# A graph network on one core: the relation rows are stored after the next turn's first fetches, and x is fetched after the edge lists

## The reference

```python
x = _layernorm(x + _L0_gnn_ref(...))   # attention over 4 heads
x = _layernorm(x + _L1_gnn_ref(...))   # mean of messages, own term, relu, norm
# layer 2: softmax over the edges that leave a node, weighted sum at the target
e = ei_all[idx_i] + ej_all[idx_j]
e = jnp.where(e > 0, e, 0.01 * e)
alpha = _segment_softmax(e, idx_j, n)
out = relu(jax.ops.segment_sum(alpha[:, None] * x[idx_j], idx_i, n))
x = _layernorm(x + out)
# layer 3: a matrix for each of 4 relations, maximum at the target, own term
hr = x_src @ weight[r] + bias[r]        # r = relation of the edge
agg = jax.ops.segment_max(msg, dst, n)
x = _layernorm(x + (x @ weight[-1] + bias[-1] + agg))
```

## Time and profile before

| | us |
|---|---|
| runs: median of 3 (lowest, highest) | 4865.99 (4858.77, 4874.44) |
| profiled execution, its own time | 4846.01 |
| its span | 4844.2 |
| busy in the span: PE, DVE, ACT, POOL | 2474.6, 2187.0, 836.0, 3265.1 |
| second part of layer2 | about 2866 to 3684 |
| edge_lists | 0 to about 56 |

### The profile page before, as it was taken

The page is one execution under the profiler, slowest core; times in us unless marked ns, Lnnn a source line. Parts: engine busy times, 40 slices in busy tenths (PEclk is TensorE's granted clock), DMA queues, the critical chain, the costliest instruction groups (busy, mean ns, idle before and its releaser), DMA issues. The chain is left out here.

```text
span 4844.2 us, 67984 instructions
## 1 busy us (share of the span) xinstructions
PE 2474.6 (51%) x17617; PEld 2281.1 (47%) x17617; DVE 2187.0 (45%) x5635; ACT 836.0 (17%) x2497; POOL 3265.1 (67%) x3391
## 2 busy tenths in 40 slices
PE   1555555554344444443999986655654333333331
PEld 1444444443333333332999985544543333333331
DVE  4555555554122222223666666656653222222224
ACT  0122222221000000000444430000001111111112
POOL 2777777775777777774677776444432777777775
PEclk7555555555555555555555556666666555565565
DMA  4333333332222223232566666555553444444453
GB/s 106 80 82 81 80 80 80 81 81 53 54 55 55 55 55 56 55 55 58 175 179 183 178 203 201 174 187 171 168 183 94 130 130 130 130 132 132 132 132 95
DMA packets 421571, 550.23 MB, mean 114 GB/s; under 512 B 110747, under 2 KB 280175, under 8 KB 421343
## 3 DMA queue, kind: packets, MB, share of 16 engines
q1 hardware_dynamic: 306098, 319.68, 21.7%
q0 software_dynamic: 108064, 223.24, 20.6%
q10 hardware_dynamic: 7344, 6.61, 0.4%
HBM read 412.21 MB, written 138.30 MB: 114 GB/s over the span
## 5 line engine op out<-in xcount | busy, mean ns | idle before, releaser
L521 POOL DMA_INDIRECT G<-table,IC x2496 | 2367.3, 948 | 896.4 <-issue 787.3
L2397 POOL DMA_INDIRECT G<-table,IC x832 | 839.6, 1009 | 526.5 <-issue 370.5
L1358 PE MATMUL PS<-SEL,G 128*128 128x96 f32 x1664 | 384.2, 426 | 534.5 <-DMA G<-table,IC 528.1
L1358 PEld LDWEIGHTS PS<-SEL,G 128*128 128x128 f32 x1664 | 362.4, 330 | 557.2 <-issue 550.9
L2801 DVE TENSOR_TENSOR_SCAN GW<-BIG,GW,PS 128x512 f32<-128x512 bf16 x208 | 266.2, 1280 | 780.9 <-PE PS L2776 771.2
L1030 PE MATMUL PS<-SEL,GW 128*128 128x96 f32 x1664 | 385.9, 426 | 405.7 <-DVEq L1093 405.7
L1030 PEld LDWEIGHTS PS<-SEL,GW 128*128 128x128 f32 x1664 | 360.8, 329 | 415.3 <-DVEq L1093 415.3
L2776 PE MATMUL PS<-IDENT,G 128*128 128x128 f32 x832 | 204.7, 428 | 680.3 <-DMA G<-table,IC 680.3
L2776 PEld LDWEIGHTS PS<-IDENT,G 128*128 128x128 f32 x832 | 163.2, 223 | 717.1 <-DMA G<-table,IC 528.5
L2405 PE MATMUL PS<-BIG 128*128 128x49 f32 x1680 | 377.6, 412 | 1.1 <-ACT BIG L2345 1.1
L2405 PEld LDWEIGHTS PS<-BIG 128*128 128x128 f32 x1680 | 371.3, 334 | 1.2 <-ACT BIG L2345 1.2
(11 more groups left out here) (309 smaller groups left out, 3894.5 us busy)
## 6 DMA issues: line engine op xcount, KB each, us to landing
running_max<-BIG SPq DMA_DIRECT2D x105, 512.0 KB
GW<-source_in_block SPq DMA_DIRECT2D x209, 256.0 KB
G<-table,IC POOLq DMA_INDIRECT x3328, 2.5
rows_ahead<-G SPq DMA_DIRECT2D x104, 512.0 KB
ROWSF<-edge_places SPq DMA_DIRECT2D x209, 192.0 KB
BIG<-run_mask SPq DMA_DIRECT2D x104, 256.0 KB, 4.6
ROWSF<-rows_ahead SPq DMA_DIRECT2D x26, 512.0 KB
SELTF<-rows_ahead SPq DMA_DIRECT2D x26, 512.0 KB, 6.4
```

What stands on the lines that cost most here:

```text
L521: pool.indirect_dma_start(out=G[:, b, u, 0:width], out_offset=None, in_=table, in_offset=bass.IndirectOffsetOnAxis(ap=IC[:, b * U + u:b * ...
L1358: last = t.matmul(PS[q][:, 0:W], G[:, b, u, 0:D], SEL[:, q, u, :], start=u == 0, stop=u == U - 1)
L2397: pool.indirect_dma_start(out=GS[:, b, u, :], out_offset=None, in_=T2, in_offset=bass.IndirectOffsetOnAxis(ap=IC[:, b * U + u:b * U + u + ...
```

## The change

Two edits. In `edge_lists` ACT waits until the four edge-list tiles have landed before it fetches x. In the second part of `layer2` the store of a chunk moves from the end of its turn to the middle of the next one, behind that turn's groups 0 and 1 and its spills; the last chunk is stored after the loop. The two stores of a chunk and the wait ahead of them are the same as before.

```diff
@@ edge_lists, ACT
                     act.wait_ge(x_in, 48)
+                    act.wait_ge(rows_in, 64)
                     act.dma_start(XBUF[:, 0:N], xT).then_inc(x_in, 16)
@@ layer2
-            def sp_laps(sp, first, end, nodes0, nodes1):
+            def sp_laps(sp, first, end, nodes):
...
                             if b == 1:
                                 for j in range(2):
                                     spill(sp, lap * 4 + 52 + 2 * h + j, 2 * h + j, lap + 13)
-                        if (nodes0, nodes1)[h]:
-                            n, blk = chunk_of(turn)
-                            store_rows3(sp, S, n, blk, 2)
+                                if nodes:
+                                    n, blk = chunk_of(lap * 2 + h - 1)
+                                    store_rows3(sp, S, n, blk, 2)
...
-                        sp_laps(sp, 0, 1, False, False)
-                        sp_laps(sp, 1, 2, False, True)
-                        sp_laps(sp, 2, 13, True, True)
+                        sp_laps(sp, 0, 2, False)
+                        sp_laps(sp, 2, 13, True)
+                        store_rows3(sp, S, CHUNKS - 1, LEFT - 2, 2)
                         sp.wait_ge(S.stored, 32 * CHUNKS + 32)
```

## The result

| | before | after |
|---|---|---|
| runs: median (lowest, highest), us | 4863.99 (4858.77, 4874.44) | 4669.68 (4666.10, 4672.76) |
| after / before, 95% interval | | 0.9598 (0.9586 to 0.9610) |
| profiled execution, us | 4846.01 | 4666.10 |

The medians are 194.3 us apart, the two profiled executions 179.9 us (that of before lies 12.8 us under the quickest of its four runs, that of after is the quickest of its own). The changed kernel has one line more ahead of layer2, so L2498 of before is L2499 here, L890 is L891, L936 is L937.

What follows compares the result with a forecast made beforehand. Bound: DVE's own chain plus a list fetch queued on SP behind the wait for that chain's end. 182.3 - 4.5 + 4.2 = 182.0 us saved, set against the 4866.0 median: 4684 us, range 4652 to 4730.

Steps and rivals of the forecast that it cites:

- (a): Second part of layer2: with the list of group 0 issued earlier, all 22 list waits go, 182.3 us gained.
- (f): Lap ends in layer2: a jump hidden by the wait now shows, 0.41 x 11 = 4.5 us lost.
- (e): DVE's L890 in layer2 waits for PE's relation products: no change taken, bounds 44 us lost to 19.3 gained.
- (c): Layer2, row fetch and list of group 2 now behind the store: no cost, at least 1.9 us in hand.
- (d): Layer2 spills go out later, at about 3244: no cost, POOL has nearly 5 us in hand.
- (g, 0.73 forecast: Layer2, more bytes in less time: DMA engines' share rises from 0.55 to 0.73, cost taken as 0.
- x (4.2 us): edge_lists, x fetched later: SP passes the padding wait at 14.0 instead of 18.2, 4.2 us gained, between 0 and 5.4.
- need the same 10.8 us: edge_lists: after the padding the four lists take as long as before, 10.8 us (18.20 to 29.01).
- rival 1: PE's clock stays low in layer2, L890 waits 2.9 us every turn: saving falls to 138, 4728 us; chance 0.10.
- (2): Layer2, POOL cannot gather while its next spill lands: turns of 27.3 us, 132 saved, 4734 us; chance 0.06.
- (3): Layer2, group 2's list behind the store's wait comes too late: slower, 4939 us at a 22 us landing; chance 0.04.
- (4): Layer2, group 0's list waits for something else, say the buffer half; only the x edit counts: 4862 us; chance 0.03.

Runs made afterwards that it cites:

- The x experiment: Changed kernel with x fetched once the padding has landed, beside the list loads: 0.9681 of the kernel before on the slow chip; DVE starts on the lists at 30.09 us.

## Why the prediction was right, and which steps were off

**The list waits (a): right.** 182.3 us were to go, and no list wait is left in the turns with a chunk. The second part went from 801.8 to 619.0 us. Taking off the list waits (182.3 and 2.3 before, 1.6 after) and those for PE's products inside it (19.3 and 18.4) leaves 597.9 before and 599.0 after. The kernel with only the store moved leaves 597.3 (606.5 less 2.0 and 7.2), and the changed kernel in its second profile 597.5 (621.7 less 2.4 and 21.8): nothing else of any size changed.

**The lap's jump (f): wrong.** By the same numbers the jump costs nothing that can be told (597.3 to 599.0 without the list waits that hid it, 597.9 with them); 4.5 us had been charged from a single step of the earlier trace rows. One pair of rows with another releaser in it was too little for a term.

**PE's clock and L890 (e): right in this profile, but it is a spread.** The wait is 20.9 us after (18.4 of them between the first and the last L2513) and was 19.3 before. Rows of L891 in the changed kernel show the two kinds of turn:

```profile
3205.74 1.28 DVE L891 TENSOR_TENSOR BIG<-PS,BIG 128x512 f32<-128x512 f32 x2
...
3232.06 1.29 DVE L891 TENSOR_TENSOR BIG<-PS,BIG 128x512 f32<-128x512 f32 x2 [2.37 <-PE PS L882]
...
3305.16 1.28 DVE L891 TENSOR_TENSOR BIG<-PS,BIG 128x512 f32<-128x512 f32 x2
...
3329.04 1.28 DVE L891 TENSOR_TENSOR BIG<-PS,BIG 128x512 f32<-128x512 f32 x2
```

A turn with the wait takes 26.3 us, one without 23.9. The granted clock is 0.67 in the first (3207 to 3233 us) and 0.79 in the second (3305 to 3329), so the wait goes with the clock. In the kernel with only the store moved the wait was 7.2 us in 4 turns inside the part (mean clock 0.75), and its second part was 12.5 us shorter than the changed kernel's for it: 606.5 us. That was the exception: with the store from ACT, behind group 0, behind group 2 and in the second profile of the changed kernel it was 17 to 22 us in all. The rule of the Trainium skill ("TensorE: Matmul & The Clock Gate", "HAM oscillation") bears out halfway: with the hole gone the mean clock rose from 0.65 to 0.73, but ten turns still waited, so the 19.3 us it would have given did not come. The hole is not all that the clock depends on: with the products on PE and ACT it was 0.82.

**The fetches behind the wait (c): right**, with the slack confirmed from both sides: 27.0 us lost where it is 1 us short, nothing gained one group later. The spills (d) and the DMA share (g, 0.73 forecast, 0.77 found) cost nothing; POOL waits 68.5 us for the spills, 3.8 us each time in 18 turns, as it may.

**x (4.2 us): the direction right, the size too small, 7.0 us.** Against the one profile that the prediction had, the padding gained 3.9 of the 4.2 forecast. The step that failed is that the four lists "need the same 10.8 us": they took 7.9 (14.27 to 22.12). What had held them up in the kernel before is not shown; x had landed at 19.1 (9.33 + 9.8), 0.9 us after they began. Nor is this split fixed: in the three other profiles with x early the lists took 7.8 to 8.1 us as well, and the padding lost the whole 8.2 to 8.6 us. The 18.20 from which the working starts was one execution's number. The x experiment showed that the two can't be had apart. The rule of the Trainium skill to issue early ("DMA: Bandwidth & Descriptors", "Rules for kernel authors") would have kept x first; fetched last, x is still on time, and 6.9 us are gained.

**From the profile to the median: off by 14 us.** The sum against the profiled execution gave 4664.0, and it took 4666.1. The forecast of 4684 set the same saving against the median of the runs, 20 us above the profiled execution of before; the changed kernel's median is only 3.6 us above its own. The measured saving is 194.3 us where 182.0 were forecast: 2.8 of the 12.3 are x, 4.5 the jump; where the remaining 5 come from is not shown, and they lie within what the wait for PE alone varies by (18.4 us here, 7.2 us with only the store moved). That the profiled execution came within 2.1 us of its 4664.0 is in part luck: the two parts that the change touches gained 7.8 us more than forecast (189.8 against 182.0), and the stages that it does not touch took 9.9 us longer. The other 2 of the 14 are the median of before itself, 4863.99 here and 4865.99 in the runs shown ahead of the prediction.

**The rivals.** PE at its low clock throughout (rival 1) did not happen. Spills and gathers as a ring (2) would have shown turns of 27.3 us, and those without a wait for PE take 23.9. The list of group 2 too late (3) is a real mechanism at the wrong distance: the store one group earlier brings it about. That the buffer half would hold the list up (4) is out; the list goes out 10.4 us ahead.

## What to carry to other kernels

In a queue that issues both fetches and stores, ask for each wait what stands behind it: a wait for the end of a turn, ahead of the first fetch of the next, exposes that fetch's whole latency in every turn, however small the store is. Move the wait behind the fetches that are needed first, or to an idle queue (here the two are worth the same), and check the first fetch left behind it by issue time plus landing against the time of its need; one group of difference was worth 27 us. A large fetch that is needed late should wait for the small ones that are needed first, all of them.

## What was not expected of the hardware

- With x beside them, SP needed 7.00 us to issue one list load of 448 KB that took 0.56 us to issue without x: the cost appears as a long issue on the queue, not only as a long landing.
- A matmul with one row of contraction and 512 columns in float32 took as long as one with 128 rows (1.12 and 1.05 us for two records in the trace, which are one such matmul).
- The same program took 4855, 4861 and 6393 us on three chips. On the slow one the gather and scan stages were longer and edge_lists was not; why stays open.
